# A two-layer graph transformer on one core: expert gates scored on rows without their norm, one stage from the experts' rows to the second node tables, and both mixtures folded

## The reference

```python
xn = layernorm(x)                                   # layer 0
x = x + gat_cell(xn, edges) + mix0(xn)              # 1 head of attention over edges, then an LSTM-like cell
x = x + experts0(layernorm(x))                      # 8 experts, the best 2, weighted by their softmax
xn = layernorm(x)                                   # layer 1
x = x + gat8(xn, edges) + mix1(xn)                  # 8 heads over edges, elu
x = x + experts1(layernorm(x))                      # 8 experts, the best 2, unweighted

# mix0: k, v normed per head, kv = k^T v / n (per head), then
out = q @ kv + x ; return gelu(out @ w1 + b1) @ w2 + b2 + x
# mix1: k = softmax(k, over nodes); context = k^T v (per head)
out = (q @ context) * sigmoid(gelu(ln(x) @ Wg1 + bg1) @ Wg2 + bg2) ; return out @ Wproj + bproj
# experts: logits = x @ gate_w + gate_b; top 2 of 8; y = gelu(x @ W1[e] + b1[e]) @ W2[e] + b2[e]
```

## Time and profile before

| what | us |
|---|---|
| median of 3 runs | 2380.77 (2379.01 to 2397.41) |
| the profiled execution, its own time | 2377.53 |
| its span | 2374.7 |
| PE busy, DVE busy, POOL busy, ACT busy | 1718.0, 1252.3, 1067.8, 587.6 |
| mean granted clock of PE | 0.842 |
| first edge sums, 100 to 774 us: PE busy, granted clock | 494.05, 0.85 |
| second edge sums, 1276 to 1990 us: the same | 515.79, 0.86 |

### The profile page before, as it was taken

One profiled execution on the slowest core, in us unless ns is written; L12 is line 12 of the kernel. 1 busy time (PEld: TensorE's weight loads), 2 busy tenths in 40 slices (PEclk: granted clock), 3 DMA queues, 4 the chain that ended last, 5 costly groups with the idle time before them and its releaser, 6 DMA issues. The chain is left out here.

```text
span 2374.7 us, 36095 instructions
## 1 busy us (share of the span) xinstructions
PE 1718.0 (72%) x9958; PEld 1428.1 (60%) x9958; DVE 1252.3 (53%) x3643; ACT 587.6 (25%) x1948; POOL 1067.8 (45%) x1066
## 2 busy tenths in 40 slices
PE   4266777678778977999455475777778784679991
PEld 3244555567666556999334364566667573579991
DVE  6346666454456666222485364656667578642223
ACT  3122121123222531333122121223222123213330
POOL 0466656655462000555203665757656453025550
PEclk9678898889899975999777787889989898569996
DMA  5533322322221033776513332323223220437776
GB/s 100 141 87 88 81 77 80 81 79 73 61 79 41 0 122 102 213 213 210 149 44 84 87 82 77 90 74 92 74 67 81 58 72 1 144 110 212 213 205 171
DMA packets 157984, 244.23 MB, mean 103 GB/s; under 512 B 53353, under 2 KB 95852, under 8 KB 157542
## 3 DMA queue, kind: packets, MB, share of 16 engines
q0 software_dynamic: 48384, 134.19, 20.6%
q1 hardware_dynamic: 107290, 106.27, 15.8%
q10 hardware_dynamic: 2124, 1.54, 0.3%
HBM read 210.48 MB, written 31.21 MB: 102 GB/s over the span
## 5 line engine op out<-in xcount | busy, mean ns | idle before, releaser
L701 POOL DMA_INDIRECT es_rows<-table,eall x784 | 823.0, 1050 | 710.2 <-SPq L690 296.8
L780 ACT ACTIVATE es_oneT<-bank 125x512 bf16<-125x512 f32 x244 | 145.6, 597 | 988.9 <-remote 460.6
L719 PE MATMUL bank<-es_rows,es_won 128*125 x976 | 284.0, 441 | 44.7 <-DVE es_won L832 34.0
L719 PE MATMUL bank<-es_msg,es_one 128*125 128x264 f32 x976 | 271.0, 425 | 35.3 <-DVE es_msg L835 24.1
L719 PEld LDWEIGHTS bank<-es_rows,es_won 128*125 128x125 f32 x976 | 200.8, 217 | 83.0 <-issue 50.2
L727 PEld LDWEIGHTS bank<-es_stage,es_oneT 125*128 125x128 bf16 x976 | 57.6, 101 | 309.8 <-ACT es_oneT L780 163.2
L727 PE MATMUL bank<-es_stage,es_oneT 125*128 125x6 bf16 (+1 forms) x976 | 65.0, 179 | 247.1 <-ACT es_oneT L780 145.4
L719 PEld LDWEIGHTS bank<-es_msg,es_one 128*125 128x125 f32 x976 | 192.0, 208 | 79.4 <-DVE es_msg L835 32.4
L825 DVE TENSOR_TENSOR es_one<-nodes,ends 128x500 bf16 (+1 forms) x244 | 166.1, 681 | 109.4 <-issue 109.2
L1371 DVE TENSOR_TENSOR ffn_shared<-bank,ffn_b2s 128x256 f32<-128x256 f32 x112 | 47.6, 425 | 331.9 <-PE bank L1212 179.2
L1202 PE MATMUL bank<-ffn_xbT,ffn_w 128*128 128x128 f32 x1792 | 222.5, 278 | 0.0
(11 more groups left out here) (390 smaller groups left out, 2703.6 us busy)
## 6 DMA issues: line engine op xcount, KB each, us to landing
ffn_w<-in_L_ffn_W SPq DMA_DIRECT2D x112, 512.0 KB
es_rows<-table,eall POOLq DMA_INDIRECT x784
ffn_w<-yrows SPq DMA_DIRECT2D x20, 560.0 KB
ffn_w<-in_L_ffn_W SPq DMA_DIRECT2D x2, 4096.0 KB
xrows<-acc SPq DMA_DIRECT2D x10, 560.0 KB
table<-acc SPq DMA_DIRECT2D x5, 577.5 KB
table<-acc SPq DMA_DIRECT2D x5, 564.4 KB
out_x<-xs SPq DMA_DIRECT2D x5, 560.0 KB
```

The source lines that it names most:

```text
L701: pool.indirect_dma_start(rows[:, q % R, w, :], None, m.table[H], bass.IndirectOffsetOnAxis(ap=m.eall[:, at:at + 1], axis=0)).then_inc(gat ...
L719: ins = pe.matmul(sum_banks[p % 2][0:P, 0:W], left, right, start=(w == 0), stop=(w == BW - 1))
L780: a.activation(oneT[:, p % 2, :], turn_bank[0:P, :], ACT.Copy).then_inc(kept, 1)
```

## The change

1. **Gates.** A new class `Logits` turns the rows of `m.xs` without their norm (through bank 6) and multiplies them by the gate's columns (into bank 7, which keeps 25 x 8 logits and the columns' sums) inside graph_attention0, now unrolled, and inside finish1. The experts stage has no `normalise` stage, no turn and no score: it forms mean and rstd, corrects the 200 logits in four instructions, adds the bias, chooses for all 25 tiles at once and ranks once. The normed rows for the gather are written by ACT.
2. **combine_tables1** takes the place of the combine at ffn0's end, score_columns1, normalise "ln1" and node_tables "nt1": POOL weighs and adds the first expert row, DVE adds the second one and makes statistics, norms come in three parts (after tiles 10, 18, 25), and one product of 336 columns per tile gives table, scores and the gate's pre-activation, which is rescaled at the end, turned and bent.
3. **Mix0**: wq is transposed in step 2; after the sums (step 65 to 70) wq, kv and w1 are joined into one matrix, added to w1; a tile then needs one product (`hide`, steps 71 to 95) and the output (steps 89 to 113).
4. **Mix1**: the context sums k against the rows `m.xs` (256 columns) instead of v; each tile one step (31 to 55); in steps 61 to 66 the sums are turned, multiplied by wv, masked, multiplied by wq; the output takes 2 steps for each tile from step 67 on. `es1` turns its flags as bf16 too: `upper` takes the upper halves of the float32 flags.
5. **Row order** of `xrows` and `yrows`: node rows lie as (p t), so 5 tiles of one partition are one piece of 5 KB in `yrows`.

The core of the diff (file headers, buffers and the engines' parts that follow from these left out):

```diff
-                        else:
-                            ins = pe.transpose(at, one[:, p % O, w, :], m.ident[:, :])
+                        flags = one[:, p % O, w, :] if H == 1 else upper(one[:, p % O, w, :])
+                        ins = pe.matmul(at, flags, ident[:, :], start=True, stop=True)
...
+    def turn(self, pe, t, added):
+        pe.wait_ge(added, t + 1)
+        if t >= 1:
+            pe.wait_ge(self.kept, t)
+        for k in range(KD):
+            ins = pe.transpose(self.m.bank[6][:, k * 128:k * 128 + P], self.m.xs[:, t, k * 128:(k + 1) * 128], self.m.ident[0:P, 0:P])
+        ins.then_inc(self.turned, 1)
+
+    def keep(self, a, t):
+        a.wait_ge(self.turned, t + 1)
+        if t >= 2:
+            a.wait_ge(self.scored, t - 1)
+        a.activation(self.rowT[:, t % 2, :, :], by_feature(self.m.bank[6]), ACT.Copy).then_inc(self.kept, 1)
+
+    def score(self, pe, t):
+        pe.wait_ge(self.kept, t + 1)
+        for k in range(KD):
+            ins = pe.matmul(self.m.bank[7][0:P, t * NE:(t + 1) * NE], self.rowT[:, t % 2, k, :], self.gws[:, k, :], start=(k == 0), stop=(k == KD - 1))
+        ins.then_inc(self.scored, 1)
...
-                    copy_rows(sp, m.xrows.rearrange("(t p) d -> p t d", p=P)[:, i:i + C, :], m.acc[:, i:i + C, 0:D], rows_stored)
+                    copy_rows(sp, m.xrows.rearrange("(p t) d -> p t d", p=P)[:, i:i + C, :], m.acc[:, i:i + C, 0:D], rows_stored)
...
+                pe.wait_ge(masked, 1)
+                at = both[:, :, :].rearrange("p t e -> p (t e)")
+                pe.matmul(rank_bank[0:P, 0:NT * NE], m.before[:, :], at, start=True, stop=True)
+                pe.matmul(total_bank[:, 0:NT * NE], m.ones[0:P, :], at, start=True, stop=True).then_inc(ranked, 1)
...
+                a.wait_ge(scaled, 1)
                 for t in range(NT):
-                    a.wait_ge(turned, t + 1)
-                    if t >= 2:
-                        a.wait_ge(logged, t - 1)
-                    a.activation(xst[:, t % 2, :, :], by_feature(m.bank[t % 2]), ACT.Copy).then_inc(staged, 1)
+                    a.activation(m.acc[:, t, 0:D], m.xs[:, t, :], ACT.Identity, bias=shift[:, t:t + 1], scale=m.rstd[:, t:t + 1]).then_inc(normed, 1)
...
+                k.link(v.tensor_copy(gsum[:, :], m.bank[7][0:P, NT * NE:(NT + 1) * NE]))
+                k.link(v.tensor_tensor(lg[:, :, :], over(m.mean[:, :], NT), gsum[:, :].unsqueeze(1).to_broadcast([P, NT, NE]), ALU.mult))
+                k.link(v.tensor_tensor(lg[:, :, :], m.bank[7][0:P, 0:NT * NE].rearrange("p (t e) -> p t e", e=NE), lg[:, :, :], ALU.subtract))
+                k.link(v.tensor_tensor(lg[:, :, :], lg[:, :, :], over(m.rstd[:, :], NT), ALU.mult))
...
+                k.link(v.tensor_tensor(lg[:, :, :], lg[:, :, :], gbs[:, :].unsqueeze(1).to_broadcast([P, NT, NE]), ALU.add))
...
+                src = lg[:, :, :]
+                for x in range(2):
+                    k.link(v.tensor_reduce(best[:, x, :], src, AX.X, ALU.max))
+                    k.link(v.tensor_tensor(eq[:, :, :], src, over(best[:, x, :], NT), ALU.is_equal))
+                    k.link(v.scalar_tensor_tensor(eq[:, :, :], eq[:, :, :], -100.0, ie[0:P, :].unsqueeze(1).to_broadcast([P, NT, NE]),
+                                                  ALU.mult, ALU.add))
+                    k.link(v.tensor_reduce(low[:, :], eq[:, :, :], AX.X, ALU.min))
+                    k.link(v.tensor_tensor(one[x][:, :, :], eq[:, :, :], over(low[:, :], NT), ALU.is_equal))
+                    if x == 0:
+                        k.link(v.scalar_tensor_tensor(mask[:, :, :], one[0][:, :, :], -BIG, src, ALU.mult, ALU.add))
+                        src = mask[:, :, :]
+                v.tensor_tensor(both[:, :, :], one[0][:, :, :], one[1][:, :, :], ALU.add).then_inc(masked, 1)
...
+def combine_tables1(nc, m):
...
+                        u, y = t // C, yy[:, t // C % 2, 0, t % C, :]
+                        if t % C == 0:
+                            pool.wait_ge(yy_in[u % 2], 64 * (u // 2 + 1))
+                        pool.tensor_tensor(y, y, m.cw[:, 0, t:t + 1].to_broadcast([P, D]), ALU.mult).then_inc(weighed, 1)
+                    if t >= 1:
+                        pool.wait_ge(weighed, t)
+                        pool.tensor_tensor(m.xs[:, t - 1, :], m.xs[:, t - 1, :], yy[:, (t - 1) // C % 2, 0, (t - 1) % C, :], ALU.add).then_inc(first, 1)
...
+                def add(t):
+                    u = t // C
+                    if t % C == 0:
+                        v.wait_ge(yy_in[u % 2], 64 * (u // 2 + 1))
+                    v.wait_ge(first, t + 1)
+                    v.scalar_tensor_tensor(m.xs[:, t, :], yy[:, u % 2, 1, t % C, :], m.cw[:, 1, t:t + 1], m.xs[:, t, :],
+                                           ALU.mult, ALU.add).then_inc(used, 1)
...
+                def norms(lo, hi):
+                    at = slice(lo, hi)
+                    v.wait_ge(counted, hi)
+                    moments(v, k, m.stats[:, at, :], m.mean[:, at], m.var[:, at], half[:, at], other[:, at])
+                    root_of(v, k, m.rstd[:, at], shifted[:, at], m.var[:, at], bits[:, at], half[:, at])
+                    k.link(v.scalar_tensor_tensor(shift[:, at], m.mean[:, at], -1.0, m.rstd[:, at], ALU.mult, ALU.mult))
...
+                for t in range(NT):
+                    add(t)
+                    if t >= 1 and t not in ENDS:
+                        stats(t - 1)
+                    if done < ready:
+                        norm(done)
+                        done += 1
+                    if t + 1 in ENDS:
+                        stats(t)
+                        norms(ready, t + 1)
+                        ready = t + 1
...
+                gates = tail[:, :, HEADS:]
+                v.tensor_tensor(gates, gates, rho[:, :].unsqueeze(2).to_broadcast([P, NT, GH]), ALU.mult).then_inc(gated, 1)
...
+                        for b in range(KD):
+                            ins = pe.matmul(m.bank[2 + u % 2][0:P, 0:W], m.xT[:, b, tile_cols(u)], m.nodew[:, b, 0:W], start=(b == 0), stop=(b == KD - 1))
+                        ins.then_inc(rowed, 1)
...
+        if i == self.FOLD:
+            pe.wait_ge(self.mixer, 1)
+            for k in range(KD):
+                ins = pe.transpose(m.bank[7][:, k * 128:(k + 1) * 128], m.kv[:, k, :], m.ident[:, :])
...
+            for k in range(KD):
+                ins = pe.matmul(m.bank[4][:, k * D:(k + 1) * D], self.kvT[:, k, :], m.w1[:, k, :], start=True, stop=True)
+            ins.then_inc(self.joined, 1)
...
+                    pe.matmul(m.bank[7][:, b * D:(b + 1) * D], m.wq[:, k, b * 128:(b + 1) * 128], self.after[:, k, :],
+                              start=(k == 0), stop=(k == KD - 1))
...
+                pe.wait_ge(self.ready, 2)
+            else:
+                pe.wait_ge(self.hkept, t)
...
-                    ins = pe.matmul(m.bank[4][:, o * 128:o * 128 + P], m.wq[:, k, o * 128:(o + 1) * 128], m.xT[:, k, tile_cols(t)],
+                    ins = pe.matmul(total[:, o * 128:o * 128 + P], m.w1[:, k, o * 128:(o + 1) * 128], m.xT[:, k, tile_cols(t)],
                                     start=(k == 0), stop=(k == KD - 1))
-            ins.then_inc(self.queried, 1)
+            ins.then_inc(self.hidden, 1)
...
-                ins = pe.matmul(total[:, k * 128:(k + 1) * 128], self.ek[:, s, k * 128:(k + 1) * 128], self.vv[:, s, k * 128:(k + 1) * 128],
+                ins = pe.matmul(total[:, k * D:(k + 1) * D], self.ek[:, s, k * 128:(k + 1) * 128], m.xs[:, t, :],
...
-                pe.transpose(m.bank[4][0:P, k * 128:(k + 1) * 128], self.ekT[:, s, k, :], m.ident[:, :])
-            for k in range(KD):
-                ins = pe.matmul(m.bank[7][0:P, 0:D], m.xT[:, k, tile_cols(t)], m.wqkv[:, k, 2 * D:3 * D], start=(k == 0), stop=(k == KD - 1))
+                ins = pe.transpose(m.bank[4 + 3 * (t % 2)][0:P, k * 128:(k + 1) * 128], self.ekT[:, s, k, :], m.ident[:, :])
...
+        if i == self.FOLD:
+            pe.wait_ge(self.levelled, 1)
+            for k in range(KD):
+                for b in range(KD):
+                    at = k * D + b * 128
+                    ins = pe.transpose(m.bank[7][:, at:at + 128], self.sums[:, k, b * 128:(b + 1) * 128], m.ident[:, :])
...
+                for b in range(KD):
+                    ins = pe.matmul(m.bank[4][:, k * 128:(k + 1) * 128], self.sumsT[:, k, b * 128:(b + 1) * 128],
+                                    m.wqkv[:, b, 2 * D + k * 128:2 * D + (k + 1) * 128], start=(b == 0), stop=(b == KD - 1))
+            ins.then_inc(self.crossed, 1)
...
+                    at = b * D + k * 128
+                    ins = pe.matmul(m.bank[7][:, at:at + 128], self.wqT[:, k, b * 128:(b + 1) * 128], m.kv[:, k, :], start=True, stop=True)
+            ins.then_inc(self.mapped, 1)
...
-        for t in self.output(i, 2):
-            s = t % 2
-            pe.wait_ge(self.qkept, t + 1)
-            if t >= 1:
-                pe.wait_ge(self.gone, t)
-            for k in range(KD):
```

(11 more changed lines are left out.)

646 lines of the change are left out of this document (311 added, 335 removed).

## The result

The changed kernel takes 2315.25 us (median of 4 runs, 2296.29 to 2325.05) where the kernel before takes 2389.09 (now 4 runs, 2379.01 to 2398.50): a ratio of 0.970, 95% interval 0.965 to 0.975. The forecast of 2209 and its range, 2145 to 2290, lay too low. The profiled execution, the fastest of the four, took 2296.29 us, its span is 2294.6, 80.1 shorter than the one before (the medians lie 74 apart); its mean clock is 0.840 against 0.842.

A forecast was written before the change was run, and what follows sets the result against it. The prediction took PE's side work to bound much of the edge sums, with stages outside them following one another. Its terms, -33 - 33 + 18 + 6 - 24 - 40 - 55 - 8 = -169, took 2377.5 to 2209 us; range 2145 to 2290.

The forecast's parts named there:

- There PE's side work is passed on whole: Edge sums: from steps without side work to the output's, PE gains 1.71 us a step and the step 2.23.
- -40: First edge sums: folding Mix0 removes 47.4 us of PE and adds 6; forecast -40, bounds -10 to -75.
- -55: Second edge sums: Mix1 folded and flags turned as bf16 give -67 of PE, four fifths taken: -55 (-15 to -95).
- Rival (a): Edge sums don't pass PE's time on; foldings give about 15 instead of 95: 2289; chance 0.22, including in-between cases.
- the clock rival (c): PE's granted clock falls: 2252 at 0.82, slower from 0.69, 2470 at 0.65; chance 0.06, half of it mild.
- the 95: Both edge sums: the gain forecast from the two foldings with the bf16 turn, 40 and 55 us.
- 4 x 1.050 = 4.20 us a block: Edge sums: gathers occupy POOL that long, 98 blocks, 412 us a stage, well under the stage's 680 to 715.
- Gates: Experts stages: gates moved out, both rows chosen at 869.8 instead of 903.14; -33 us in each stage.
- Cell: Cell, PE-bound: the gate work added there costs +18 us; window 95 to 105 us, PE busy over 90%.
- finish1: finish1: gate work added on a cold PE, 42 us against 35, so +6 (+2 to +12).
- combine_tables1: New stage before the second edge sums: bound by DVE, edge sums start at 1249 to 1253; -24 (-35 to -8).
- 80 to 90 us from the last scatter: Sign for the new stage: the time from the last scatter to the second edge sums in the changed kernel.

The follow-up runs named there:

- e14: The kernel before, unaltered, on a chip without the long waits: 2116.10 us.
- e1: The changed kernel, with POOL gathering only the first 8 of 98 blocks in both edge sums (old rows reused): 1993.82 us.
- e2: The kernel before, with POOL gathering only the first 8 of 98 blocks in both edge sums: 2081.29 us.
- e13: The changed kernel, unaltered, on a chip without the long waits: 2022.37 us, 0.9585 of the kernel before.
- e17: The changed kernel, all gathers, with the second edge sums' w_proj product and DVE's last addition one step later: 2004.54 us, 0.949 of the kernel before.
- e7: The changed kernel, all gathers, with PE's turn of the flags ahead of the side work in both edge sums: 2291.67 us, 0.9625 of the kernel before.
- e8: The changed kernel with Mix0 and Mix1 of the kernel before (unfolded), flags still turned as bf16: 2324.26 us, 0.9757 of the kernel before.
- e9: The changed kernel without gathers after the eighth block, DVE weighing only half of es_msg after the second step of the second edge sums: 1901.15 us.
- e18: As e17, and in the second edge sums the turn of the flags stands before the side work: 2002.64 us, 0.948 of the kernel before.
- e3: The changed kernel with two gathers instead of four for each block after the first eight: 1998.25 us.
- e4: The changed kernel with blocks after the eighth loaded by SP as plain loads of the same size instead of POOL's gathers: 1990.48 us.
- e11: The changed kernel with POOL running at most 6 blocks ahead instead of 8, all work kept: 2027.34 us.
- e15: The same edit as e11, run again beside the unaltered changed kernel: 2024.49 us, 0.960 of the kernel before.
- e10: The changed kernel with all gathers, DVE weighing only half of es_msg after the second step of the second edge sums: 1976.96 us.
- e16: The same edit as e10, run again beside the unaltered kernels: 1975.77 us.

## Why the prediction was wrong, and where it was right

**The failed step.** "There PE's side work is passed on whole", read from the steps without side work against the output's, and the terms -40 and -55 built on it. It fails in four ways.

- The 3.36 us of the steps without side work were DVE's. Its busy time, 14.97 of 16.80 us, stood in the same line of the earlier trace rows as PE's 14.35, and without gathers these steps take 16.7 us whether PE is busy 14.5 or 12.1. A step bounded by one engine against a step bounded by another says nothing about a rate of passing on. Moreover, five steps were too few: in that stretch the kernel before happened to have no long wait, and the changed one has four (27.1 us against 16.8).
- In the output both engines were near the bound. The kernel before had PE busy 187 and DVE 158 of 203.4 us (e14), with the side work of nine steps spread over 5 tiles. The changed kernel had less of PE, but with all three side products in one step of two, and the two engines waited for each other in turns: 4.73 us a step became 4.88. Rival (a), that the edge sums don't pass PE's time on, came true in size (2289, against 2296 in the profiled execution), but not for its reason. It named ACT's long waits and the keys' steps; without the long waits (e1 against e2, e13 against e14) the gain was 19 to 20 us. So that its figure was met is in part luck. That it isn't the foldings as such, e17 shows: with `w_proj`'s product one step later the output gives 4.39. Even so the second edge sums take 549.5 us against e14's 568.8, 19 of the 55.
- PE's removed 67 us were only 35, as what stayed got dearer: 425 to 446 ns for a sum, at a clock of 0.88 instead of 0.92 in the output. It was the same on the chips without long waits (486.14 to 451.41 from e14 to e13) and more so without gathers (472.10 to 448.72 from e2 to e1). That is a mild form of the clock rival (c). In the whole the clock stood still, and its strong form didn't come.
- Where the long waits are absent, the second edge sums' steps before the output wait for rows: from the fifth copy to the 67th e14 takes 303.7 us and e13 302.2, 42 and 44 more than e2 and e1 without gathers (261.4 and 258.1), and DVE's waits for rows are 48.9 and 44.4. POOL's gathers set the pace there, and nothing taken off PE can show; without gathers it gave 3 us.

For the chip of the two profiles themselves, which has the long waits, these four were read from runs elsewhere. How much of the 95 each of them takes there beside the waits stays open; what is shown is that the waits aren't what hides the gain, since it doesn't come without them.

In the first edge sums half of the -40 came where the long waits are absent (22 us, e14 against e13, with POOL's gathers as the cap), and a third (14) in the profiled executions. There the steps with `hide` took 5.1 us each where the query's took 5.74 and 4.7 was foretold.

**A floor taken too low.** "4 x 1.050 = 4.20 us a block", 412 us a stage, left out the 0.30 us between two gathers. With them a stage's gathers take 392 x 1.35 = 529 us. At 690 us a stage it didn't matter, as POOL still waited 158.6 us for freed slots; where the long waits are absent it binds. There the second edge sums' gathers take 433.7 us and the gaps 119 in e13, and 438.9 and 119 in e17, whose 122 copies take 549.5 us and start 15 after the first gather.

**Gates**: right. The choice was ready at 868.2 (forecast 869.8), and the first gather came 47 us after the experts' first instruction in both stages (857.15 to 904.05, 1985.98 to 2033.10), as forecast; the preparation's DMAs fitted in. **Cell**: 102 us with PE 95.29 busy, as foretold (95 to 105); -33 + 18 = -15 became -19. **finish1**: from its first DVE instruction to the experts' first one 40.8 us instead of 36.1, +5 where +6 was forecast; with the gates -27 became -28. **combine_tables1**: -24 became -19. The data came at 1140.43, 19.6 us after the last scatter's issue instead of 10.8 before: the Block's end cost 8.8 us where 6 were taken. DVE's two-input instruction there took 746 ns on average and not 580, 4 us more over 25; the rest came out 2 us shorter. The sign "80 to 90 us from the last scatter" doesn't follow from the term itself: from the last scatter to the first gather of the edge sums it was 121 us before, so 97 were forecast, and 101 were measured. **Row order**: -8 became -2.5. DVE's five waits for `yrows` sum to 21.1 us against 23.2.

On ports: the forecast took 0.58 for a two-input addition of DVE beside POOL, from the earlier trace rows. In the changed kernel's finish1 the addition of L2095 takes double its time while POOL divides (until 1965.3), and its plain time after:

```profile
1950.38 0.83 DVE L2095 SCALAR_TENSOR_TENSOR xs<-acc,xs 125x256 f32<-125x256 f32 x1
1951.13 0.83 DVE L2092 TENSOR_TENSOR xs<-xs,fin_e 125x256 f32<-125x256 f32 x1
...
1975.41 0.42 DVE L2095 SCALAR_TENSOR_TENSOR xs<-acc,xs 125x256 f32<-125x256 f32 x1
```

0.58 was a mean over both. The Trainium skill ("SBUF — State Buffer", Who interferes with whom) says that a DVE instruction with two SBUF inputs contends with a GpSimd instruction that reads SBUF, through an exclusive lock on a shared port pair. The 0.83 agrees; but L2092, with two inputs too, takes 0.50 us in most of the same stretch and 0.40 after it, so not every one waits out a whole instruction of POOL. The -14 that the prediction worked out by that rule was too dear: -19 came.

## What to carry to other kernels

A step that two engines share costs what the slower chain of the two costs in that step, not the mean: before counting work taken off one engine, add up the other's instructions in one step, from the time line, with its waits. When the work of a pipelined step is thinned, look anew at where what stays stands; here the same instructions, one product and one addition moved by a step, gave 21 us. The floor of an engine that only issues gathers is their busy time with the gaps between them, 1.41 us each here and not 1.11, and it can hold part of a stage while another engine holds the rest. And a difference of step lengths is a rate only if both kinds of step are bound by the same engine and there are enough of them to hold their share of the rare long waits.

## What the runs showed of the hardware

**Signals that come late beside a run of gathers.** In the two kernels' own profiles and in e7 and e8, ACT waits 211 to 283 us in an edge stage for a releaser that isn't on the core's engines. On the chips of e9 to e18, with all the gathers, it never does, and the kernel before takes 2107 to 2109 us instead of 2346 to 2389. The time line of the longest such wait in the changed kernel's second edge sums:

```profile
1582.79 0.95 POOL L546 DMA_INDIRECT es_rows<-table,eall  x1 [0.30 <-issue]
...
1585.10 0.40 PE L583 MATMUL bank<-es_ident,es_one 128*125 128x128 bf16 x4
...
1592.03 0.36 DVE L687 TENSOR_REDUCE es_near<-bank 128x64 f32<-128x192 f32 x1 [6.56 <-remote]
...
1596.60 0.94 POOL L546 DMA_INDIRECT es_rows<-table,eall  x1 [0.30 <-issue]
1600.52 0.60 ACT L623 ACTIVATE es_oneT<-bank 125x512 bf16<-125x512 f32 x1 [16.28 <-remote]
```

The four turns that the copy waits for are done at 1585.5; the copy starts 15 us later, 3 us after the end of a row of gathers that POOL issued with nothing but 0.30 us between them. DVE's `es_near`, which waits for PE's scores of 1584.3, comes at 1592.0. With the waits gone, by e1, e3 and e4, both stages are some 150 us shorter. So such a wait needs indirect gathers from POOL close behind one another: the first 32 of a stage bring it even in e1 and e3, but pairs of gathers with pauses between them hardly do (after the first four steps e3 has two such waits, 8 us, in its first edge sums and none in the second), nor do plain loads of the same bytes. That PE's signals are held up is what the rows suggest; what holds them, and why only on some chips, stays open, and a chip with the waits wasn't there to try POOL's pace on (e11, e15).

**A gather costs more beside a busier DVE.** On the chips without long waits a gather of the second edge sums holds POOL for 1.11 to 1.14 us on average (e11 to e15, e17, e18) and for 1.01 in e10 and e16, where DVE's `es_msg` is half as wide; in the first edge sums it is 1.03. So less work on DVE shortened POOL's as well, by 38 us in the stage (433.7 to 395.4). Which of DVE's instructions does it wasn't tried.

**A pause of DVE every eighth step.** Once in eight steps DVE stands up to 3.8 us before `es_one` with nothing that it waits for (in the changed kernel's second edge sums 50.7 us in 15 times); in the kernel's text DVE reads the numbers of the next eight steps into registers there. That is up to 50 us a stage of the engine that bounds its output's steps. It was read, not tried.
